# Gated cross-attention with a top-2 expert layer: the prologue in another order

## The reference

```python
q, k, v = layernorm(x) @ wq + bq, ctx @ wk + bk, ctx @ wv + bv      # split into 16 heads
scores = q @ k.T / sqrt(8) + mask + local_window_mask(32, 16 global)
x = x + tanh(g_xattn) * (softmax(scores) @ v @ wo + bo)
h = layernorm(x)
p = top2(softmax(h @ gate_w)), normalised
x = x + tanh(g_ffn) * sum_i p_i * (silu(h @ w1[i]) * (h @ w3[i])) @ w2[i]
```

## Time and profile before

| what | value |
|---|---|
| median of 3 runs | 459.47 us (458.91 to 459.83) |
| span of the profiled execution | 458.1 us |
| PE busy | 407.4 us, 89% of the span |
| DVE, ACT, POOL busy | 290.9, 239.6, 259.4 us |
| first attention matmul on PE (L853) | 53.60 us |

### The profile page before, as it was taken

The page is one execution under the profiler, slowest core; times in us unless marked ns, Lnnn a source line. Parts: engine busy times, 40 slices in busy tenths (PEclk is TensorE's granted clock), DMA queues, the critical chain, the costliest instruction groups (busy, mean ns, idle before and its releaser), DMA issues.

```text
span 458.1 us, 14422 instructions
## 1 busy us (share of the span) xinstructions
PE 407.4 (89%) x4547; PEld 360.1 (79%) x4548; DVE 290.9 (64%) x786; ACT 239.6 (52%) x564; POOL 259.4 (57%) x312
## 2 busy tenths in 40 slices
PE   2879979999999998997879899988999999999970
PEld 1647658877777776776669799888999999999960
DVE  3876798887888887889546368544444554554420
ACT  2758506667677675766666534233444444444430
POOL 5743554334654737473646568776666665655560
PEclk9989979999999999999999999999999999999995
DMA  7964557457766666485223233334444343333235
GB/s 215 279 123 94 96 96 185 90 105 113 170 147 136 152 134 161 106 216 169 65 69 75 45 52 48 54 67 61 69 70 58 44 54 46 46 47 40 24 29 189
DMA packets 74783, 46.24 MB, mean 101 GB/s; under 512 B 8608, under 2 KB 71490, under 8 KB 74562
## 3 DMA queue, kind: packets, MB, share of 16 engines
q1 hardware_dynamic: 59072, 34.84, 33.2%
q0 software_dynamic: 12272, 8.92, 14.9%
q10 hardware_dynamic: 3392, 1.88, 1.7%
HBM read 18.12 MB, written 14.20 MB: 71 GB/s over the span
## 4 chain that ended last, share of the span: by engine, by line
PE 62%; DMA 9%; issue 7%; DVE 6%; ACT 6%; POOL 4%; ACTq 2%; POOLq 1%; DVEq 0%
PE ps_scores L1612 20%; PE ps_max_scores L1620 10%; DMA sums_scratch<-yt,xg 8%; PE ps_values L897 7%; PE ps_max_scores L853 6%; PE ps_scores L883 5%; PE ps_scores L837 3%; PE ps_max_scores L837 2%; POOL expert_rows_scratch L1328 2%; PE ps_out L921 1%; ACT xn L474 1%; DVE rsplit L1119 1%; ACT w_all L464 1%; DVE qkf L558 1%; POOL sums_scratch L1733 1%
## 5 line engine op out<-in xcount | busy, mean ns | idle before, releaser
L1733 POOL DMA_INDIRECT sums_scratch<-yt,xg x71 | 115.9, 1633 | 66.9 <-DMA sums_scratch<-yt,xg 28.1
L1612 PE MATMUL ps_scores<-xgT,qs 128*128 128x128 f32 x1136 | 141.1, 278 | 5.1 <-ACT xgT L1658 3.8
L1612 PEld LDWEIGHTS ps_scores<-xgT,qs 128*128 128x128 f32 x1136 | 134.1, 194 | 7.1 <-ACT xgT L1658 4.5
L1699 DVE TENSOR_TENSOR qs<-qs,ps_scores 128x512 f32<-128x512 f32 x71 | 48.8, 688 | 88.4 <-PE ps_scores L1612 70.5
L1119 DVE TENSOR_REDUCE rsplit<-ps_max_scores 128x4 f32<-128x512 f32 x128 | 84.8, 685 | 15.0 <-PE ps_max_scores L837 11.2
L1328 POOL DMA_INDIRECT expert_rows_scratch<-xr,pos x64 | 66.4, 1037 | 25.6 <-issue 13.1
L1620 PE MATMUL ps_max_scores<-w_all,qs 128*128 x568 | 75.6, 276 | 2.8 <-ACT yt L1669 2.3
L1620 PEld LDWEIGHTS ps_max_scores<-w_all,qs 128*128 128x128 f32 x568 | 69.0, 192 | 3.8 <-issue 3.6
L1027 ACT ACTIVATE pT<-ps_scores 128x1024 f32<-128x1024 f32 x64 | 62.0, 1022 | 18.1 <-PE ps_scores L837 17.8
L1662 ACT ACTIVATE qs<-ps_scores 128x512 f32<-128x512 f32 x71 | 42.3, 596 | 30.3 <-PE ps_scores L1612 30.3
L1669 ACT ACTIVATE yt<-ps_max_scores,xg 128x128 f32<-128x128 f32 x71 | 26.1, 368 | 60.4 <-PE ps_max_scores L1620 40.4
(11 more groups left out here) (202 smaller groups left out, 527.8 us busy)
## 6 DMA issues: line engine op xcount, KB each, us to landing
qs<-w_all SPq DMA_DIRECT2D x96, 64.0 KB
ks<-w_all SPq DMA_DIRECT2D x96, 64.0 KB
w_all<-in_L_ffn_w_dram SPq DMA_DIRECT2D x24, 256.0 KB
xg<-expert_rows_scratch SPq DMA_DIRECT2D x71, 65.0 KB, 1.9
xs<-in_x_dram SPq DMA_DIRECT2D x4, 512.0 KB, 5.6
sums_scratch<-xs SPq DMA_DIRECT2D x8, 256.0 KB, 4.5
sums_scratch<-yt,xg POOLq DMA_INDIRECT x71, 3.3
expert_rows_scratch<-fill SPq DMA_DIRECT2D x16, 65.0 KB, 2.5
```

The source lines that it names most:

```text
L1612: ins = nc.tensor.matmul(bank[u % 2][:, c * P:(c + 1) * P], w13[:, u % 2, n, c * P:(c + 1) * P], xgT[:], start=True, stop=True)
L1699: nc.vector.tensor_tensor(hidT[:, u % 2], act_s[:, u % 2], ps_b[u % 2], ALU.mult).then_inc(hid_ready, 1)
L1733: pool.indirect_dma_start(out=z_d, out_offset=bass.IndirectOffsetOnAxis(ap=xg_u[:, u, X_IDX:X_IDX + 1], axis=0), in_=yt[:, u % YRING], in_ ...
```

## The change

The chunks of `x` become 4, 4, 8, 8 and 8 batches, and one load of `x` more is issued. The square root's table is loaded early on ACT by an instruction on a dummy tile `warm`. Seven small loads (`wo`, `bo`, `gate_w`, `bv`, mask, two gates) go from ACT's queue to SP's. The biases get a semaphore of their own. PE projects q and k of group 0 ahead of the router's and group 1's transposes, and those of group 1 ahead of group 2's. `copy_turned(0)` is split around `normalise(0)`, and `first_part(0)` stands ahead of `normalise(2)`. `statistics` of the later chunks stand behind `take_gates`. On POOL the mask's parts come behind the constants. SP copies the constant rows of `ks` behind the loads of group 0.

```diff
-        XCH = 4
+        CHUNKS = (GB, GB, 2 * GB, 2 * GB, 2 * GB)
+        def chunk_of(g):
+            return 0 if g == 0 else 1 + g // 2
...
             load_x(0)
             load_ctx(0)
+            load_x(1)
             load_ctx(1)
-            load_x(1)
+            load_x(2)
+            sp.dma_start(wo_x[:, 0:D], wo).then_inc(router_loaded, 16)
+            sp.dma_start(bo_x[:, 0:D], bo.partition_broadcast(P)).then_inc(router_loaded, 16)
+            sp.dma_start(gate_sb[:], gate_w).then_inc(router_loaded, 16)
             sp.wait_ge(win_ready, WIN_SPANS + 2)
...
             load_ctx(2)
-            load_x(2)
+            sp.dma_start(bv_row[:], bv.partition_broadcast(P)).then_inc(small_loaded, 16)
+            sp.dma_start(mrow[:], mask_in).then_inc(small_loaded, 16)
+            sp.dma_start(gates[:, 0:1], g_xattn.partition_broadcast(P)).then_inc(small_loaded, 16)
+            sp.dma_start(gates[:, 1:2], g_ffn.partition_broadcast(P)).then_inc(small_loaded, 16)
+            load_x(3)
             load_ctx(3)
-            load_x(3)
+            load_x(4)
...
+            copy_rows(0)
+            sp.wait_ge(fixed_ready, 2)
             sp.wait_ge(mpart_stored, 16)
-            for g in range(2):
-                sp.wait_ge(parts_ready, g + 1)
-                if g == 1:
-                    sp.wait_ge(tile_copied, 16 * TILE_COPIES)
-                for p in range(2):
-                    load_half(sp, g, p)
+            sp.wait_ge(parts_ready, 1)
+            for p in range(2):
+                load_half(sp, 0, p)
+            copy_rows(1)
+            sp.wait_ge(tile_copied, 16 * TILE_COPIES)
+            sp.wait_ge(parts_ready, 2)
+            for p in range(2):
+                load_half(sp, 1, p)
...
+            load_table(act, ACT.Sqrt)
...
+            std(0)
+            copy_ctx(0, 0)
             normalise(0, 0)
+            std(1)
+            copy_xn(0, 0)
+            act.wait_ge(bias_loaded, 16 * BIASES)
+            nc.scalar.mul(bqs_col[:], bq_col[:], SCALE).then_inc(gates_ready, 1)
             normalise(1, 1)
-            std(1)
-            act.wait_ge(gates_ready, 1)
-            copy_turned(0, 0)
-
+            std(2)
             act.wait_ge(router_turned, 1)
...
             copy_turned(1, 1)
+            act.wait_ge(gates_ready, 1)
+            first_part(0, 0)
             normalise(2, 0)
-            first_part(0, 0)
             act.wait_ge(mpart_ready, 1)
...
             copy_turned(2, 0)
-            std(2)
             normalise(3, 1)
             first_part(1, 1)
             copy_turned(3, 1)
             std(3)
             normalise(4, 0)
             first_part(2, 0)
+            std(4)
...
             for g in range(NG - 2):
                 split(g, g % 2)
                 bias_v(g)
+                take_gates(g)
                 if g < 2:
+                    statistics(g + 3)
+                if 0 < g < 3:
                     invert(g + 2)
-                if g == 0:
-                    statistics(3)
-                take_gates(g)
...
+            def second():
+                turn_router()
+                turn(1, 1)
+            project(0, 0, second)
+            project_gates(0, 0)
+            project(1, 1, lambda: turn(2, 0))
+            project_gates(1, 1)
+            turn(3, 1)
```

More of the change, by code:

```diff
@@ L188, in build, with chunk @@
         idx_f = sb("idx_f", [P, 2, GB])
-        XCH = 4
-        x_loaded = [sem(f"x_loaded{i}") for i in range(XCH)]
+        CHUNKS = (GB, GB, 2 * GB, 2 * GB, 2 * GB)
+        assert sum(CHUNKS) == B
+        def chunk(i):
+            return slice(sum(CHUNKS[:i]), sum(CHUNKS[:i + 1]))
+        def chunk_of(g):
+            return 0 if g == 0 else 1 + g // 2
+        x_loaded = [sem(f"x_loaded{i}") for i in range(len(CHUNKS))]
         proj_loaded = sem("proj_loaded")
+        bias_loaded = sem("bias_loaded")
         by_dim_ready = sem("by_dim_ready")
@@ L199, in build @@
         ident_ready = sem("ident_ready")
+        warm_ready = sem("warm_ready")
         pool_step = sem("pool_step")
@@ L235, in build @@
         gates_taken = sem("gates_taken")
-        PROJ = 3 + 2
+        PROJ = 3
+        BIASES = 2
         SMALL = 4
@@ L286, in load_x @@
             def load_x(i):
-                n = B // XCH
-                sp.dma_start(xs[:, i * n:(i + 1) * n], x_v[:, i * n:(i + 1) * n]).then_inc(x_loaded[i], 16)
+                sp.dma_start(xs[:, chunk(i)], x_v[:, chunk(i)]).then_inc(x_loaded[i], 16)
             def load_ctx(g):
@@ L427, in project_gpsimd, with load_table @@
             return last_part
+        def load_table(act, function):
+            act.wait_ge(warm_ready, 1)
+            nc.scalar.activation(warm[:, 1:2], warm[:, 0:1], function)
         def project_scalar(act):
@@ L568, in project_vector @@
             statistics(1)
+            invert(1)
+            statistics(2)
             dve.wait_ge(fixed_loaded, 16 * 4)
             fix(0)
-            invert(1)
+            invert(2)
             fix(1)
-            statistics(2)
             dve.wait_ge(small_loaded, 16 * SMALL)
@@ L586, in project_tensor, with turn @@
         def project_tensor(pe):
-            def turn(g, u, between=None):
+            def turn(g, u):
                 if not (isinstance(g, int) and g == 0):
@@ L594, in turn @@
                 ins.then_inc(ctx_turned, 1)
-                if between:
-                    between()
                 pe.wait_ge(xn_written, (g + 1) * GB)
@@ L600, in turn, with project @@
                 ins.then_inc(xn_turned, 1)
-            def project(g, u):
+            def project(g, u, between=None):
                 pe.wait_ge(turned_copied, g * 2 + 2)
@@ L609, in project @@
                 nc.tensor.matmul(bank[:, 1], w_by_dim["k"][:], ctxT[:, u], start=True, stop=True).then_inc(qk_done, 1)
+                if between:
+                    between()
                 if not (isinstance(g, int) and g == 0):
@@ L636, in project_tensor @@
             pe.wait_ge(ident_ready, 2)
-            turn(0, 0, turn_router)
-            turn(1, 1)
+            turn(0, 0)
             pe.wait_ge(proj_loaded, 16 * PROJ)
             pe.wait_ge(by_dim_ready, 2)
-            for g in range(NG - 2):
+            def second():
[6 more added lines that the diff above has]
+            turn(3, 1)
+            for g in range(2, NG - 2):
                 project(g, g % 2)
```

70 lines of the change are left out of this document (31 added, 39 removed).

## The result

The changed kernel takes 469.49 us (median of four runs, 468.66 to 603.15). The kernel before took 459.65 us beside it. Every median in this document is of all runs, while every ratio leaves out each run that lies more than 1.5% above the fastest of its kernel, here the one of 603.15, and where the runs lie far apart (f1: 6 of 12 left out, e3: 4 of 10, e4: 3 of 10, h3: 3 of 12, i2: 2 of 6) the ratio flatters the kernel. The ratio is 1.0189 [1.0137, 1.0242]: the kernel became slower by 1.9%, about 9 us, where 458.3 us and a gain were forecast. The profiled execution took 470.02 us, with a span of 468.3 us.

What follows compares the result with a forecast made beforehand. Until the attention at 53.6 us the prologue's chain over several engines, not PE, was taken as the bound; its marks moved 0.9, then 1.2 us earlier, so 459.47 - 1.2 = 458.3 us, range 456.8 to 459.9.

Steps and rivals of the forecast that it cites:

- the last of the prediction's signs of being wrong: Sign of a wrong forecast, whole kernel: the attention starts earlier and the end does not.
- the mask's row: Rival: mask loads late in SP's queue hold ACT's copy of group 2; with the like 12%, slower, or store landing late, 460.5 to 461.
- The first group: Prologue start: first normalisation at 7.3 instead of 9.94, group 0's q and k done at 14.0 instead of 19.4.
- Group 1's transposes: PE in the prologue: router and transposes end at 17.0, bounds 14.2 to 17.5, depending on when the clock rises.
- T: Time when `xn` of group 1 is turned on PE, taken as 17.0 us.
- From T to F1: Prologue, ACT and PE from group 1's turned `xn` to the end of `first_part(1)`: 7.85 us.
- F1: End of `first_part(1)` on ACT: 25.77 us before, forecast 24.85, 0.9 earlier.
- From F1 to F3: From the end of `first_part(1)` to that of `first_part(3)`: 13.85 us instead of 14.14, ending at 38.7, 1.2 earlier.
- The price that hung on the lock: DVE's `shift` ahead of `normalise(4)`: 0.25 us, since POOL's subtraction is over; at 1.50 there would be no gain.
- The rival of held statistics: Rival: POOL's subtraction holds bn_stats of the last chunk on DVE, all 1.4 us later, 459.7 us; chance 8%.
- The rest at nothing: SP's nine more issues, its later `ks` row copies and POOL's memsets cost nothing; group 1's loads end at about 70.
- cover of 10 us is left: Group 1's loads, ending at about 70, are needed at 82.88; beyond that cover each us would cost one.

Runs made afterwards that it cites:

- f1: The change with both `ks` row copies first and the seven small loads back on ACT's queue, in its idle stretches: 464.83 us, ratio 1.0012.
- e3: The change with the `ks` rows copied between the two halves of group 0's loads: 462.67 us, ratio 1.0054.
- e4: The change with both `ks` row copies first and `invert(3)` ahead of the last chunk's statistics: 462.21 us, ratio 1.0009.
- h3: The change with `ks` rows issued by POOL, the seven small loads on ACT and the early `invert`: 464.04 us, ratio 1.0028.
- i2: The change with both `ks` row copies first and eight extra tiny loads on SP ahead of them: ratio 1.0181.
- f2: The kernel before with only the seven small loads moved to SP's queue: 459.87 us, ratio 0.9988.
- h2: The change with the six `ks` row copies issued by POOL instead of SP: 462.14 us, ratio 1.0023.
- j2: The kernel before with only SP's stream as in the change (small loads on SP, `ks` rows late), repeated on another chip: 460.11 us, ratio 1.002.
- g2: The change with expert 0's three weight loads between the `ks` row copies and the wait for their landing: 470.67 us, ratio 1.0212.
- j1: The change unaltered, run a third time against the kernel before: 473.2 us, ratio 1.0278.
- f0: The change unaltered, run again against the kernel before: 471.46 us, ratio 1.0225.
- e1: The change with the `ks` rows of both buffers copied ahead of group 0's loads, as before: 462.3 us, ratio 1.008.
- i1: The kernel before with only SP's stream as in the change (small loads on SP, `ks` rows late), first run: ratio 1.0036.
- e2: The kernel before with the `ks` rows copied behind group 0's loads, as in the change: 462.13 us, ratio 1.0071.

## Why the prediction was wrong, step by step

The mark that came true is the last of the prediction's signs of being wrong: the attention starts earlier and the end does not. No rival had SP's stream for its cause; the 14% for "slower" were given to the mask's row or the like.

- **"The first group"**: right. First normalisation at 7.14 (7.3 forecast), q and k from 10.72 to about 14.3 (10.6 to 14.0).
- **"Group 1's transposes"**: T was 16.3, not 17.0. The transposes at 15.26 and 15.70 took 0.60 us for four, as at the high level, where those at 8.84 had taken 1.12; T lies inside the bounds given. The granted clock doesn't show this rise: it reads 1.00 from 10 to 14 us as well, while the 512-column records still took 2.05 and 1.92 us.
- **"From T to F1"**: 7.7 us against 7.85, so F1 came at 24.04 instead of 24.85.
- **"From F1 to F3"**: 13.69 us against 13.85. `normalise(4)` started 5.64 behind F1 (5.75 forecast), released by `shift`. The price that hung on the lock was right: `shift` took 0.17 us with POOL's subtraction over by 28.42, against 1.50 in the earlier trace rows. The rival of held statistics did not happen: bn_stats of the last chunk took 1.64 us for eight, under that subtraction, as in the earlier trace rows.
- **The mask's row**, the rival on the slow side: it did not happen either. POOL's last step on the mask ended at 18.09 (18.7 forecast), the store was issued at 18.12, and ACT still had normalisations to do.
- **"The rest at nothing"**: this is the step that failed, in three places. First, it set group 1's loads to end "at about 70". They ended at 75.2: SP had to issue the rows for 7.25 us and wait for their landing for 4.8 us more, between the groups, and the packets then flowed slowly (1.7 us). The eight more issues (the prediction says nine) were not hidden either: SP's first copies began at 18.67 instead of 16.23; by f2, that alone costs nothing. Secondly, "cover of 10 us is left" was measured from these loads to the matmuls of group 1 alone. As far as it went it held, since PE never waited for these loads. But SP goes on behind them with the weights and group 2's loads, and ACT's `npT` stores, which every batch needs soon, share the DMA engines with them. The first thing that came late was not group 1 but `npT`, at 67.38. Thirdly, waits were priced at their length ("beyond it each us would cost one"); the one of 3.27 us cost 5.8 with the low clock behind it. What stood at nothing measured 8.7 us by batch 4.
- **The assumption that the prologue's gain is the kernel's**: it fell as well. "What the prologue gains is gained, if nothing else in it becomes late" was true only by its condition. In h2, with SP's loss nearly gone, the 2.2 us are lost again between batches 11 and 31.

What stays open: why the 512-byte packets of group 1's loads take 75 ns in the change, 62 in j2 and 50 before. That they restart together after the queues have run dry was my guess. It can't be the whole of it: the DMA share is 0.00 from 54 to 56 us in the change and in j2 alike, and g2, in which weights filled that gap, still has 64 ns; nothing shows another cause. Also open is what makes the later `npT` landings slow in h2 and h3 and not in the kernel before. What the runs show is that the place of the `ks` rows in SP's queue makes most of the loss: with the rows on POOL the changed kernel is at 1.0023. They also show that lateness, slow packets and an earlier attention come together in the dear cases, but not how much each of them adds. SP's two edits cost 0 to 0.7% in the kernel before, the change with the rows first 0.8%, and the change 1.9 to 2.8%. Why the times of f1, i2 and h3 lie so far apart stays open too, since each of them was profiled in one execution only.

## What to carry to other kernels

When a step is moved on a queue, its cover is not the time until its own data are read: follow the queue on to what stands behind it, and look which other queue's small, urgent transfers share the DMA engines with it. A start that comes earlier takes slack away from every transfer that was hidden before it; j2 against j1 shows the same order on SP's queue free in one kernel, while the other is 2.8% slower with it. And a wait of TensorE may be followed by a stretch at the lower clock level: price it at both, its length and nearly twice that (5.8 us for 3.27 here), and keep both ends for the range.

## What the runs showed of the hardware

- Behind PE waits of 1.97, 2.65, 3.27 and 4.89 us (j1, h2, the change, f0) the granted clock fell to 0.50 for some us; behind those of 2.91 and 2.88 us (j1) and 2.81 us (i2) it stayed at 1.00. A long wait isn't even needed. In the kernel before it fell at about 60.5 us, with no PE wait above 1.06 us near it; these two stretches show what PE did ahead of the fall and at the low level. What decides the runs do not show.

```profile
58.00:60.00 2.00, 0.94 (x13) 0.70 (x11) 1.97 (x5) 0.00 (x0) 0.29 (x1) 1.00 0.62 85
62.00:64.00 2.00, 1.12 (x7) 0.68 (x8) 1.90 (x4) 0.26 (x1) 1.92 (x4) 0.50 0.62 97
```

- At the start of the program the granted clock reads 1.00 while the matmuls still run at half speed (the change, 10 to 14 us); there the level is read from the durations.
- Stores of `npT` (12 KB), issued by ACT, landed 5.7, 7.3 and 10 us after their issue while SP's 64 KB loads and, for the last, its 256 KB weights were in flight (the change); the mask's store, of 24 KB, took 6.2 us in the earlier trace rows and 4.1 in the change.
- Packets of the same group's loads took 40 to 50 ns (h2, e1, e4, the kernel before), 57 to 64 (i1, j2, e2, g2) and 75 ns (the change) between 58 and 66 us, with SP's queue at 46 to 62% of the DMA engines.
